# A per-sample gate kernel: order of the control products, split squares, earlier group copy, regrouped sums

## The reference, cut to what matters

```python
def _L0_conv_ref(x, W1, W3):
    x = relu(x)
    avg_region = mean(x, (2, 3)); peak_region = max(x, (2, 3))
    x = where(peak_region - avg_region < 0.5, 0.0, x)
    cmax = max(x, axis=1); cmean = mean(x, axis=1)
    bb = 1.0 - exp(-abs(cmax - cmean))
    x = bb * x
    x_max = max(x, (2, 3)); pooled = mean(x, (2, 3))
    control1 = sigmoid(pooled @ W1.T)
    control3 = relu(pooled @ W3.T); control3 = where(control3 < 1.0, 1.2, control3)
    thres = control1 * control3 * x_max
    return where(x < thres, 0.0, x)
x = x + _L0_conv_ref(_gn(x), L0_conv_W1, L0_conv_W3)
```

## Time and profile before

| what | value |
|---|---|
| three runs | 1778.58, 1784.53, 1799.36 us (median 1784.53) |
| the profiled execution | 1780.24 us, its span 1778.4 us |
| PE busy | 1303.4 us (73%) |
| DVE busy | 1460.9 us (82%) |
| ACT busy | 1306.6 us (73%) |
| POOL busy | 610.6 us (34%) |
| HBM traffic | 310.38 MB read, 205.52 MB written, 290 GB/s over the span |
| mean granted TensorE clock | 0.843 of full speed |

### The profile page before, as it was taken

The page is one execution under the profiler, slowest core; times in us unless marked ns, Lnnn a source line. Parts: engine busy times, 40 slices in busy tenths (PEclk is TensorE's granted clock), DMA queues, the critical chain, the costliest instruction groups (busy, mean ns, idle before and its releaser), DMA issues.

```text
span 1778.4 us, 45243 instructions
## 1 busy us (share of the span) xinstructions
PE 1303.4 (73%) x19616; PEld 1080.2 (61%) x19616; DVE 1460.9 (82%) x2192; ACT 1306.6 (73%) x1921; POOL 610.6 (34%) x446
## 2 busy tenths in 40 slices
PE   4888776788876778767688777678777688777761
PEld 3766655666665666655576655566655566656660
DVE  2588887988887988888888887888887887888987
ACT  5678777777787878777767787777787767777821
POOL 0043233443233444223443233443233442233430
PEclk8898888998888898888888888898878887888885
DMA  9259989999999899998989999989999988899973
GB/s 396 87 162 301 319 315 320 281 296 297 312 330 336 277 285 306 302 329 320 287 263 296 307 330 332 283 277 296 301 330 329 279 265 269 315 329 343 296 228 145
DMA packets 93418, 518.86 MB, mean 292 GB/s; under 512 B 10272, under 2 KB 10272, under 8 KB 93216
## 3 DMA queue, kind: packets, MB, share of 16 engines
q1 hardware_dynamic: 75360, 416.38, 58.4%
q0 software_dynamic: 17856, 99.56, 28.7%
HBM read 310.38 MB, written 205.52 MB: 290 GB/s over the span
## 4 chain that ended last, share of the span: by engine, by line
PE 29%; POOL 26%; ACT 22%; DVE 15%; issue 7%; DMA 1%; SPq 0%; DVEq 0%; ACTq 0%; POOLq 0%
POOL xs L778 23%; ACT rs L476 8%; PE ps_turn L286 7%; PE ps_gate L347 7%; ACT xs L476 7%; PE ps_gate L322 6%; PE ps_gate L294 6%; DVE xs L670 6%; ACT rs L451 5%; DVE rs L670 4%; DVE max_and_mean L622 2%; POOL rstd L757 2%; DMA xs<-in_x 1%; PE ps_gate L356 1%; DVE xs L737 1%
## 5 line engine op out<-in xcount | busy, mean ns | idle before, releaser
L622 DVE TENSOR_REDUCE max_and_mean<-ps_turn 128x2 f32<-128x1024 f32 x384 | 466.0, 1220 | 201.3 <-PE ps_turn L286 200.6
L286 PE MATMUL ps_turn<-ident,xs 128*128 128x128 f32 (+1 forms) x1600 | 358.8, 310 | 177.7 <-DVE max_and_mean L622 112.3
L769 POOL DMA_DIRECT2D xs<-in_x x124 | 111.6, 968 | 940.0 <-DVE xs L670 837.0
L778 POOL TENSOR_TENSOR xs<-xs,rs 128x1568 f32<-128x1568 f32 x124 | 433.3, 3531 | 1.9 <-DVE rs L670 1.9
L286 PEld LDWEIGHTS ps_turn<-ident,xs 128*128 128x128 f32 (+1 forms) x1600 | 204.5, 153 | 311.5 <-DVE max_and_mean L622 155.2
L312 PE MATMUL ps_gate<-ident,bb 128*128 128x128 f32 (+1 forms) x1600 | 273.4, 333 | 153.2 <-ACT bb L469 144.0
L425 ACT ACTIVATE scratch<-xs 128x3136 bf16<-128x3136 f32 x128 | 360.2, 2814 | 7.8 <-DMA xs<-in_x 2.8
L312 PEld LDWEIGHTS ps_gate<-ident,bb 128*128 128x128 f32 (+1 forms) x1600 | 249.6, 239 | 173.4 <-DVE ymax_parts L639 157.7
L286 PE MATMUL ps_turn<-ident,rs 128*128 128x128 f32 (+1 forms) x1600 | 341.3, 299 | 6.0 <-issue 6.0
L639 DVE CUSTOM_DVE_ANT_0 xs<-xs,ps_gate 128x768 f32<-128x768 f32 (+1 forms) x256 | 243.3, 959 | 45.1 <-PE ps_gate L312 45.0
L451 ACT ACTIVATE xs<-xs,shift,rstd 128x3136 f32<-128x3136 f32 x64 | 191.9, 2999 | 100.0 <-POOL shift L761 93.3
(11 more groups left out here) (80 smaller groups left out, 991.9 us busy)
## 6 DMA issues: line engine op xcount, KB each, us to landing
xs<-in_x SPq DMA_DIRECT2D x260, 784.0 KB, 13.7
out<-xs SPq DMA_DIRECT2D x256, 784.0 KB, 8.2
xs<-in_x POOLq DMA_DIRECT2D x124, 784.0 KB, 11.1
rs<-in_L_conv_W SPq DMA_DIRECT2D x2, 1024.0 KB, 18.7
```

The source lines that it names most:

```text
L286: mm = pe.transpose(ps_turn[0:w, n % 2, b - 2 * i, P * t:P * (t + 1)], r_tile(s, t)[:, P * b:P * b + w], ident[:, :])
L622: ins = dve.tensor_reduce(max_and_mean[:, 2 * i:2 * i + 2, 0], ps_turn[:, n % 2, :, :], AX.X, ALU.max)
L778: pool.tensor_tensor(o, o, half(r_tile(s - 1, t), h), ALU.add).then_inc(added, 1)
```

## The change

Four edits, all of order; the arithmetic is the same except that the squares of one tile are summed in two halves.

1. On TensorE the control products of sample s - 1 stand in one piece behind fill 2 of sample s, where two of the four k stood behind fill 0 and two behind fill 1.
2. On ScalarE the squares of the first loaded tile of sample s + 1 are taken in two halves. The first half stands between `copy_control` and `control_exp`, the second behind it. The halves write the upper half of the scratch. The two partial sums lie in columns of `squares` (now one column wider), and `group_stats` gets a third matmul that adds the second one.
3. On ScalarE `copy_group(s + 1)` stands ahead of `gate_values(s, 0)`, where it stood behind it.
4. On ScalarE the second sum of y, `pool_sum(s, 0, 1)`, stands ahead of the last `relu`, where only the first one did.

```diff
@@ group_stats @@
-                pe.wait_ge(squared, T * (s + 1))
-                pe.matmul(ps_group[:, 1, :], group_avg[:, :], squares[:, :], start=True, stop=True
-                          ).then_inc(group_sums, 1)
+                pe.wait_ge(squared, (T + 1) * (s + 1))
+                first = LOAD_ORDER[0]
+                pe.matmul(ps_group[:, 1, :], group_avg[:, :], squares[:, 0:T], start=True, stop=False,
+                          skip_group_check=True)
+                pe.matmul(ps_group[:, 1, first:first + 1], group_avg[:, :], squares[:, T:T + 1],
+                          start=False, stop=True, skip_group_check=True).then_inc(group_sums, 1)
@@ TensorE, per sample @@
                 turn(s, 0)
-                if s > 0:
-                    control_products(s - 1, range(0, 2))
                 turn(s, 1)
-                if s > 0:
-                    control_products(s - 1, range(2, T))
                 turn(s, 2)
                 if s > 0:
+                    control_products(s - 1)
                     control_logits(s - 1)
@@ ScalarE @@
+            def square_half(s, h):
+                t = LOAD_ORDER[0]
+                act.wait_ge(x_loaded[s % XR][t][h], 16 * (s // XR + 1))
+                square(s, t, slice(HALF * h, HALF * (h + 1)), slice(HALF, HW), t if h == 0 else T)
@@ ScalarE, per sample @@
                 if s > 0:
                     copy_control(s - 1)
+                if has_next:
+                    square_half(s + 1, 0)
+                if s > 0:
                     control_exp(s - 1)
                 if has_next:
-                    square_tile(s + 1, 0)
+                    square_half(s + 1, 1)
                     square_tile(s + 1, 1)
...
                     row_means(s + 1)
+                    copy_group(s + 1)
                 gate_values(s, 0)
                 if has_next:
-                    copy_group(s + 1)
                     relu(s + 1, RELU_ORDER[0])
...
                 gate_values(s, 2)
-                pool_sum(s, 0, 0)
+                for t in range(2):
+                    pool_sum(s, 0, t)
                 if has_next:
                     relu(s + 1, RELU_ORDER[3])
                 gate_values(s, 3)
-                for t in range(1, T):
+                for t in range(2, T):
                     pool_sum(s, 0, t)
```

More of the change, by code:

```diff
@@ L95, in gated_sparsifier @@
         half_neg = sb("half_neg", [P, T])
-        squares = sb("squares", [P, T])
+        squares = sb("squares", [P, T + 1])
         row_sum = sb("row_sum", [P, 1])
@@ L340, in count_fails, with control_products @@
                 mm.then_inc(count_ready, 1)
-            def control_products(s, products):
-                for k in products:
+            def control_products(s):
+                for k in range(T):
                     pe.wait_ge(pooled_ready, NS * T * s + T * (NS - 1) + k + 1)
@@ L349, in control_products @@
                                        tile_position=(0, first))
-                if k == T - 1:
-                    mm.then_inc(control_rows, 1)
+                mm.then_inc(control_rows, 1)
             def control_logits(s):
@@ L413, in _ @@
                     count_fails(s + 1)
-            control_products(B - 1, range(T))
+            control_products(B - 1)
             control_logits(B - 1)
@@ L420, in _, with square @@
             junk_step = Steps(act, squared)
-            def square(s, t, cols, part):
-                n = cols.stop - cols.start
+            def square(s, t, cols, at, part):
                 junk_step.wait()
-                ins = act.activation(junk[:, 0:n], x_tile(s, t)[:, cols], ACT.Square, scale=float(HW) ** -0.5,
-                                     accum_out=squares[:, part:part + 1])
-                junk_step.step(ins)
+                junk_step.step(act.activation(junk[:, at], x_tile(s, t)[:, cols], ACT.Square,
+                                              scale=float(HW) ** -0.5, accum_out=squares[:, part:part + 1]))
+            def square_half(s, h):
+                t = LOAD_ORDER[0]
+                act.wait_ge(x_loaded[s % XR][t][h], 16 * (s // XR + 1))
+                square(s, t, slice(HALF * h, HALF * (h + 1)), slice(HALF, HW), t if h == 0 else T)
             def square_tile(s, n):
@@ L431, in square_tile @@
                 wait_loaded(act, s, t)
-                square(s, t, slice(0, HW), t)
+                square(s, t, slice(0, HW), slice(0, HW), t)
             def row_means(s):
@@ L487, in _ @@
             act.wait_ge(consts_ready, 1)
-            for n in range(T):
+            for h in range(2):
+                square_half(0, h)
+            for n in range(1, T):
                 square_tile(0, n)
```

## The result

| | before | after |
|---|---|---|
| median of the runs | 1791.42 us (1778.58 to 1799.36, 4 runs) | 1816.17 us (1815.79 to 1823.0, 4 runs) |
| profiled execution, its span | 1780.24, 1778.4 us | 1816.51, 1814.7 us |

The ratio is 1.0154 (95% interval 1.0079 to 1.0229). The change makes the kernel about 1.5% slower; the forecast was 1767 us, and even its range ended at 1790.

What follows compares the result with a forecast made beforehand. A chain once per sample was taken to bound the kernel, with TensorE waiting for instruction blocks; terms of -18.8, -4.5, -1.2, +5 and +4 us made -15.5, giving 1764.7, stated as 1767 us after adjusting towards the median; range 1745 to 1790.

Steps and rivals of the forecast that it cites:

- What bounds the kernel: Whole loop: a chain once per sample, 53.0 us a turn; about half the turns have 3 us waits for TensorE's instructions.
- Fills and products: TensorE's head of a sample: three fills ahead of the products start the copy of the control products 1.0 us earlier.
- Rival C: Head: products run at half clock, so only 0.3 us per turn is won; 1772 to 1785 us, chance 18%.
- Second sum of y ahead of the last relu: ScalarE's tail: fits its idle time; 1.5 us less of sums at the end, but fill 2 is last, so no gain.
- Group copy ahead of the gate values: ScalarE mid-turn: in long-wait turns gate values and fill 5 come later, VectorE's maximum 1.1 us, last relu 0.7 us.
- Squares in halves: ScalarE between copy and exponential: a 1.4 us half fits the idle time, delaying the exponential by at most 0.1 us.
- Position of the blocks: TensorE's sums of x: shifted instruction-block ends give 15 long waits of 3 us against 16 before; +5 us, perhaps +4 more.
- 2 + 3 + 4 us: TensorE's sums of x: costs for shifted block ends, more ends during loads, and one or two extra long waits.
- Rival D: TensorE's sums of x: 20 of 30 turns get long waits, at 3 us each; 1780 to 1797 us, chance 15%.

Runs made afterwards that it cites:

- e1: Kernel before with only the control products moved in one piece behind fill 2: 1809.87 us, ratio 1.0111.
- e2: Kernel before with only the group copy ahead of the gate values and the second sum of y ahead of the last relu: 1813.86 us, ratio 1.0144.
- e9: Kernel before with only the squares in halves, including the four added TensorE instructions per sample: 1797.54 us, ratio 1.007.
- e12: Changed kernel with spare TensorE waits in two places (block ends at 165) and GpSimd's first adding DMA behind two kept tiles: 1737.69 us, ratio 0.9743.
- e11: Kernel before with spare TensorE waits in two places, so blocks end at instruction 165 in every sample: 1749.15 us, ratio 0.9809.
- e8: Changed kernel with GpSimd's first adding DMA waiting for the second kept tile instead of the first: 1778.3 us, ratio 0.9942.
- e5: Changed kernel with spare TensorE waits ahead of the third spread, so blocks end at instruction 165 in every sample: 1783.33 us, ratio 0.9971.
- e6: e5 with 50 more instructions once at the start, so blocks end at 115 in every sample: 1866.93 us, ratio 1.0414.
- e3: Changed kernel with GpSimd's adding DMAs of sample s - 1 held until TensorE finished the sums of x of sample s + 1: 1878.31 us, ratio 1.0495.
- e13: e12 without the four edits, blocks still ending at 165: 1796.32 us, ratio 1.0045 to the kernel before.
- e14: e12 run again on the chip of e13: 1740.65 us, ratio 0.9734 to the kernel before.

## Why the prediction was wrong, point by point

- *What bounds the kernel* was right: a chain once per sample, and TensorE's waits for its next 16 KB of instructions as the difference between turns.
- *Fills and products*: the head came sooner than forecast, but this edit has little part in it. The copy came 1.35 us sooner and the first kept tile 1.73 (forecast 1.0 and 1.25). e1 gives 1.15 for the copy. But the two gains don't add: e2, without edits 1 and 2, has the copy at 4.19 and the first kept tile at 7.48, all four edits have 4.58 and 7.49. Next to edits 3 and 4, edits 1 and 2 together win nothing at the first kept tile. The clock did not fall behind: in the first 6 us after ymax its mean is 0.84 in after and 0.63 before. Rival C, that the head gives little, falls.
- *Second sum of y ahead of the last relu, "nothing more"*: wrong. e2 moves the copy by 1.74 us without edit 1. The reading that fill 2 and not ScalarE is last held only with the sum already moved.
- *Group copy ahead of the gate values, last relu 0.7 us late*: right. It is 0.63 us in the mean, as gate values follow the copy at 663.51 in after.
- *Squares in halves*: right, about 1.5 us a half; the exponential follows at once. How much of e9's 0.7% is the half squares and how much the place of the blocks is not shown.
- **Position of the blocks: the step that failed.** It counted 15 long waits of 3 us by where a block *ends* in the sums, as if that place were fixed, and put 2 + 3 + 4 us on all of it. Measured are 22 waits over 2 us, up to 4.6: 74.7 us of waits in the sums against 33.3. Behind them the granted clock is at 0.50 for 2.0 us more per turn, about 1 us of slower matmuls, for which the prediction had no term. Together they turn a gain of 1.7 us per turn in the head into a loss of 1.2 over the turn. The count for before was too high as well: 16 waits of 3 us were read out of the weight loads' row, 52.0 us with one idle time of 7.0 in it; the matmuls' row has 12 over 2 us, 31.4 us together. What it should have asked is when the fetch is *asked for*, a block earlier, against when the first adding DMA runs. The head pulls the adding DMAs forward by 1.7 us (they follow the first kept tile) but the loads only by 0.6, so it narrows the pause in which TensorE's blocks arrive quickly. The prediction saw only the difference between adding DMAs and TensorE's stretch, 0.27 us (measured 0.34); it left out the loads, in whose time TensorE now also starts.
- *Rival D* named the right mechanism, too many long waits, but by a count of 20 at 3 us, and so ended at 1797. The chance of 0.15 was far too low: the direction of the head's own effect on the waits was known (sooner adding DMAs), and only its size was not.

Open is how edits 3 and 4 share the 1.7 us of e2, and which long waits bring the clock down: in before one of 3.2 us has no stretch at 0.50 behind it and one of 2.3 us has.

## What to carry to other kernels

When work is moved forward in a loop, list what follows it automatically, DMAs above all, and what will not follow. Here the gain in the head started 3.2 MB of adding DMAs sooner against an instruction stream that has to be fetched through the same engines. Once those DMAs were held back by one more tile and the instruction blocks were given a fixed, harmless place, the same edits were worth 3%, and the version with all three (e12) is 2.6% faster than before. Most of that is not the edits': the place of the blocks, without them, gives 1.9% (e11). So compare the best version with a change against the best version without it, too.

## What the runs showed of the hardware

- By the packets' times an instruction block of TensorE is asked for when the block before it begins. Its packet started 0.9 us later (median) with the DMA engines nearly idle and about 4 us later while accumulating DMAs from GpSimd ran at some 210 GB/s with all engines full. At 256 instructions in 3.5 us that is a stall of up to 4.6 us. The Trainium skill ("Runtime: NRT & Kernel Launch", "Instruction fetch mechanics") calls such a crossing "mostly hidden"; in TensorE's dense stretch here it was hidden when asked for in the pause, nearly so when asked for while the loads ran (0.95 us in the means of the turn shown), and not once the adding DMAs ran.
- The granted clock fell from 1.00 to 0.50 around or behind 16 of 22 such waits in after and 5 of 12 in before; mean clock from 14 to 26 us after ymax: 0.97 before, 0.89 after, 0.98 in e8.
- Fifty instructions once, ahead of the loop, changed the time by 84 us (e5, e6): one wait of 1.0 to 1.9 us per turn behind the sums of x, and the clock behind it.
- GpSimd could not issue its fourth accumulating DMA (784 KB each) until 7 to 9 us after the first (e3, e13, e14), and everything queued behind it waited too.
